# Linear attention and a mixture of experts on one core: running sums over token pairs, the low part of the second input on GpSimd, and queues in a new order

## The reference

```
x = x + layernorm(attention(layernorm(x)))          # 16 heads of 8
x = x + layernorm(experts(layernorm(x)))            # one shared expert, the best 2 of 8 others

attention:  q, k, v = x @ W_qkv + b                 # q, k through elu + 1
            for each token t of a sequence:
              kv += k_t (outer) v_t;  ks += k_t     # 8 x 8 per head
              out_t = (q_t @ kv) / (q_t . ks + 1e-6)
            return out @ W_out + b_out
experts:    shared = gelu(x @ Wfc_s + b) @ Wproj_s + b
            p = softmax(x @ Wr); top 2, gates scaled to sum to 1
            return shared + sum over the two of gate * (gelu(x @ Wfc[e] + b) @ Wproj[e] + b)
```

## Time and profile before

| | us |
|---|---|
| median of 3 runs | 409.97 |
| lowest and highest | 406.25, 412.97 |
| the profiled execution, its own time | 410.09 |
| its span, first to last instruction | 408.3 |
| busy: TensorE, VectorE, ScalarE, GpSimd | 348.2, 285.7, 264.1, 258.4 |

### The profile page before, as it was taken

How to read it: one execution, slowest core, us unless ns; L and a number is a source line. 1 busy time by engine, 2 the same in 40 slices (tenths; PEclk the granted TensorE clock), 3 DMA queues, 4 the chain that set the end, 5 groups by cost and what they waited for, 6 DMA issues and landing times.

```text
span 408.3 us, 8196 instructions
## 1 busy us (share of the span) xinstructions
PE 348.2 (85%) x2523; PEld 299.0 (73%) x2530; DVE 285.7 (70%) x685; ACT 264.1 (65%) x700; POOL 258.4 (63%) x328
## 2 busy tenths in 40 slices
PE   7888498989878999888998839499999998998884
PEld 3447257887766878766787839389989998998863
DVE  4989488998978889987944504176554538777666
ACT  4959266796976859786536733256655558678665
POOL 8786675657849587593885556466654555486650
PEclk9969979999999989999899977789999999999999
DMA  6577455574462504234067325299977869988317
GB/s 201 160 210 199 86 159 112 116 210 118 136 177 70 162 27 141 79 95 127 28 189 228 106 94 171 77 245 259 310 219 226 252 223 350 308 282 244 119 55 206
DMA packets 53521, 69.17 MB, mean 169 GB/s; under 512 B 6365, under 2 KB 37386, under 8 KB 53482
## 3 DMA queue, kind: packets, MB, share of 16 engines
q1 hardware_dynamic: 47556, 58.58, 50.0%
q0 software_dynamic: 4544, 9.35, 6.6%
q10 hardware_dynamic: 1382, 0.79, 0.7%
HBM read 40.06 MB, written 18.15 MB: 143 GB/s over the span
## 4 chain that ended last, share of the span: by engine, by line
PE 35%; ACT 17%; another core or an unknown queue 11%; DVE 10%; issue 8%; POOL 6%; POOLq 1%; DVEq 0%; ACTq 0%
PE bO L1302 6%; PE bS L1523 5%; PE bA L1274 4%; PE bO L1523 4%; ACT hs L1127 3%; ACT L1018 2%; DVE w_lo L2078 2%; ACT shared L899 2%; ACT shared L891 1%; DVE SH L2027 1%; PE bT L1352 1%; POOL KV L705 1%; POOL expert_lists L681 1%; PE bV L1496 1%
## 5 line engine op out<-in xcount | busy, mean ns | idle before, releaser
L797 POOL DMA_INDIRECT expert_results<-yb,yrow x78 | 79.6, 1020 | 62.0 <-DVE yb L2110 35.8
L681 POOL DMA_INDIRECT expert_lists<-rows,pos x64 | 63.1, 985 | 23.0 <-issue 23.0
L1673 DVE TENSOR_TENSOR_SCAN KV<-bS,KV 128x1024 f32<-128x1024 bf16 x32 | 72.9, 2282 | 4.8 <-POOL KV L705 4.5
L1302 PEld LDWEIGHTS bO<-wout_rot,Z 128*128 128x128 f32 x512 | 59.8, 192 | 10.7 <-POOL Z L762 4.6
L1302 PE MATMUL bO<-wout_rot,Z 128*128 128x128 f32 x512 | 62.8, 277 | 5.7 <-POOL Z L762 2.0
L1127 ACT ACTIVATE hs<-bV,KV 128x256 f32<-128x256 f32 x56 | 22.0, 476 | 22.4 <-remote 9.8
L2102 DVE COPY yrow<-xb 128x2 int32<-128x2 int32 x24 | 5.2, 217 | 43.2 <-PE bS L1523 15.4
L1523 PE MATMUL bO<-KV,hs 128*128 128x128 f32 x232 | 30.8, 288 | 1.7 <-ACT hs L1127 1.7
L1274 PE MATMUL bA<-w2s_sb,hs 128*128 128x128 f32 x224 | 30.7, 289 | 0.0
L1523 PEld LDWEIGHTS bO<-KV,hs 128*128 128x128 f32 x232 | 28.8, 201 | 2.6 <-ACT hs L1127 2.5
L1274 PEld LDWEIGHTS bA<-w2s_sb,hs 128*128 128x128 f32 x224 | 28.7, 204 | 0.1
(11 more groups left out here) (371 smaller groups left out, 989.2 us busy)
## 6 DMA issues: line engine op xcount, KB each, us to landing
KV<-packed_weights SPq DMA_DIRECT2D x21, 578.0 KB
Z<-packed_weights SPq DMA_DIRECT2D x18, 578.0 KB
xb<-expert_lists SPq DMA_DIRECT2D x39, 129.0 KB
vr<-vr SPq DMA_DIRECT2D x16, 224.0 KB, 2.5
shared<-expert_results SPq DMA_DIRECT2D x7, 512.0 KB, 6.1
vr<-vr SPq DMA_DIRECT2D x16, 192.0 KB
vr<-vr SPq DMA_DIRECT2D x16, 160.0 KB
vr<-vr SPq DMA_DIRECT2D x16, 128.0 KB
```

The lines of the kernel that those rows point to most:

```text
L681: g.indirect_dma_start(out=lists, out_offset=bass.IndirectOffsetOnAxis(ap=pos[:, m:m + 1], axis=0), in_=rows[:, m // TILES, m % TILES, :], ...
L797: g.indirect_dma_start(out=results, out_offset=bass.IndirectOffsetOnAxis(ap=yrow[n][:, c], axis=0), in_=yb[n][:, c, :], in_offset=None).th ...
L1302: ins = t.matmul(bO[:, j * D:(j + 1) * D], Z[:, d, j * P:(j + 1) * P], wout_rot[:, d], start=False, stop=True, skip_group_check=True)
L1673: v.tensor_tensor_scan(w, ps_keep, w, 0.0, ALU.mult, ALU.add).then_inc(s["kv_sum"], 1)
```

## The change

- **Running sums over token pairs.** A scan now runs over 128 elements: its state takes in the even token of a pair and then the odd one, and is written at the odd token. The two operands are the even and the odd products, both in SBUF. One pair of diagonals takes four scans. `SUMS` has a column of zeros ahead of each sequence, and `sums_at(d)` reads for the tokens 2m and 2m + 1 the places 2m - 1 and 2m + 1. So an even token gets the sum up to the pair before it and lacks its own term, the same for all diagonals: (q . k) of its head times v. `own_terms` multiplies q and k of the even tokens, `own_sums` on TensorE adds up the features of a head (a matmul with `same_head`, 256 columns), `own_values` multiplies by v, and `own_added` adds the result to Z0. A reduction makes `same_head` once; the constants of `ps_keep` go.
- **Z2** moves from GpSimd to VectorE, and Z products are made one diagonal at a time. `out_part` takes diagonal 1 first, then 2 and 3, 0, 4 and 5, 6, 7.
- **Low part.** GpSimd subtracts `xt2_hi` from `xt2` (`rest_of_input`). The matmul and the copy on ScalarE go, and `fc` uses the low part last.
- **Rows.** The normalized rows are written straight into one of two row sets that alternate (`rows_of_step[i % 2]`), and `rows_of` copies once instead of twice, now between the second and the third gelu.
- **Order.** GpSimd makes the last key products ahead of the scatters; its eight scatters of a step are split 2, 3 and 3. ScalarE takes `squares_of_x1` ahead of `copy_queries`. Semaphores are shared out anew.

The core of the diff:

```diff
-        KV = sb("KV", [P, E, STEP])
+        SUMS = sb("SUMS", [P, E, STEP // L, L + 1])
+        KV = SUMS[:, :, :, 1:]
+        own = sb("own", [P, STEP // L, L // 2])
...
+        def evens(w):
+
+            return w.rearrange("p s (m o) -> p s m o", o=2)[:, :, :, 0]
+
+        def sums_at(d):
+
+            part = SUMS[:, d]
+            return bass.AP(part.tensor, part.offset, [part.ap[0], part.ap[1], [2, L // 2], [2, 2]])
+
+        def by_twos(w):
+
+            return w.rearrange("p (s m o) -> p s m o", s=STEP // L, o=2)
...
+            AT_END = 5
...
+            def rest_of_input(i):
+
+                pool.wait_ge(s["xt2_high"], i)
+                g.tensor_tensor(xt2_lo[:], xt2[:], xt2_hi[:].bitcast(F32), ALU.subtract).then_inc(s["xt2_lo"], 1)
...
-                if head and routed:
-                    route_gaps(i)
-                    route_chosen(i)
-                if from_on(i, 3) and head:
-                    scatters(i - 1, before_next(i - 1), 2 * TILES)
                 if isinstance(i, int) and i == 0:
                     means_late()
                 if head and not (isinstance(i, int) and i == 1):
                     last_pairs(i)
-                if not head:
-                    scatters(i - 1, before_next(i - 1), 2 * TILES)
+                if head and routed:
+                    route_gaps(i)
+                    route_chosen(i)
+                if i >= 3:
+                    scatters(i - 1, AT_END, 2 * TILES)
...
-                    g.tensor_tensor(Z[:, 0], KV[:, 0], qn[:], ALU.mult).then_inc(s["z0_ready"], 1)
+                    g.tensor_tensor(by_twos(Z[:, 0]), sums_at(0), by_twos(qn[:]), ALU.mult).then_inc(s["z0_ready"], 1)
...
-                    g.tensor_tensor(Z[:, 1], KV[:, 1], qn[:], ALU.mult).then_inc(s["z1_ready"], 1)
+                    g.tensor_tensor(by_twos(Z[:, 1]), sums_at(1), by_twos(qn[:]), ALU.mult).then_inc(s["z1_ready"], 1)
+                if tail and head:
+                    inv_std2(i)
...
-                if head:
-                    pool.wait_ge(s["kv_sum"], 4 * i + 2)
-                    g.tensor_tensor(Z[:, 2], KV[:, 2], qn[:], ALU.mult).then_inc(s["z1_ready"], 1)
...
-                if routed:
-                    scatters(i, 0 if head else 1, before_next(i) if head else 2 * TILES)
+                if head and routed:
+                    scatters(i, 0, 2)
+                if head and tail:
+                    rest_of_input(i)
+                if head and routed:
+                    scatters(i, 2, AT_END)
+                if not head:
+                    scatters(i, 1, 2 * TILES)
...
+                rows = rows_of_step[i % 2]
+                a.activation(rows[:, 1, :, 0:D], rows[:, 0, :, 0:D], ACT.Copy)
...
-                normal(2, lambda j: xn2[:, j], lambda j: Xt(i - 1, j), "xn2_ready", i)
+                    act.wait_ge(s["t2_done"], i - 2)
+                    act.wait_ge(s["rows_ready"], i - 2)
+                set_free(act, i - 1)
+                normal(2, lambda j: rows_of_step[(i - 1) % 2][:, 0, j, 0:D], lambda j: Xt(i - 1, j), "xn2_ready", i)
...
-                    gelus(i - 2, 0, CH, pair_h)
+                    gelus(i - 2, 0, 2, pair_h)
+                    rows_of(i)
+                    gelus(i - 2, 2, CH, pair_h)
...
+                if tail:
+                    squares_of_x1(i)
                 copy_queries(i)
+                if nxt and routed:
+                    a.activation(warm[:], one8, ACT.Exp)
                 if routed:
...
-                    act.wait_ge(s["t2_done"], i)
+                    second_input(i)
                     if from_on(i, 2):
                         act.wait_ge(s["fc_done"], CH * (i - 1))
-                    a.activation(xt2_hi[:], bT[:], ACT.Copy)
-                    second_input(i)
...
-                t.matmul(bank[:], hi, xt2_lo[:], start=True, stop=False)
-                t.matmul(bank[:], hi, xt2_hi[:], start=False, stop=False)
-                t.matmul(bank[:], lo, xt2_hi[:], start=False, stop=True).then_inc(s["fc_done"], 1)
+                if c == 0:
+                    pe.wait_ge(s["xt2_high"], st + 1)
+                t.matmul(bank[:], hi, xt2_hi[:], start=True, stop=False)
+                t.matmul(bank[:], lo, xt2_hi[:], start=False, stop=False)
+                if c == 0:
+                    pe.wait_ge(s["xt2_lo"], st + 1)
+                t.matmul(bank[:], hi, xt2_lo[:], start=False, stop=True).then_inc(s["fc_done"], 1)
...
+            def own_sums(st):
+
+                pe.wait_ge(s["own_ready"], st + 1)
+                t.matmul(bS[:, 0:STEP // 2], same_head[:].rearrange("p e h -> p (e h)"),
+                         own[:].rearrange("p s m -> p (s m)"), start=True, stop=True).then_inc(s["own_summed"], 1)
+
             def out_part(st, part):
                 if part == 0:
-                    pe.wait_ge(s["z0_ready"], st + 1)
-                if part in (1, 2):
-                    pe.wait_ge(s["z1_ready"], 2 * st + part)
-                if 1 < part < 5:
-                    pe.wait_ge(s["z_ready"], 3 * st + part - 1)
-
-                for d in ((0,), (1,), (2, 3), (4, 5), (6,), (7,))[part]:
+                    pe.wait_ge(s["z1_ready"], st + 1)
+                if 0 < part < 5:
+                    pe.wait_ge(s["z_ready"], 3 * st + min(part, 3))
+                if part == 2:
+                    pe.wait_ge(s["z0_whole"], st + 1)
+
...
+                if head:
+                    own_sums(i)
                 if nxt:
                     project(i + 1)
...
-                w = KV[:, 2 * part:2 * part + 2].rearrange("p a t -> p (a t)")
-                v.tensor_tensor_scan(w, ps_keep, w, 0.0, ALU.mult, ALU.add).then_inc(s["kv_sum"], 1)
+                for d in (2 * part, 2 * part + 1):
+                    for q in range(STEP // L):
+                        two = KV[:, d, q].rearrange("p (m o) -> p o m", o=2)
+                        ins = v.tensor_tensor_scan(two[:, 1], two[:, 0], two[:, 1], 0.0, ALU.add, ALU.add)
+                ins.then_inc(s["kv_sum"], 1)
+
+            def own_terms(i):
+
+                dve.wait_ge(s["qn_copied"], i + 1)
+                v.tensor_tensor(own[:], evens(seqs(qn[:])), evens(seqs(keys)), ALU.mult).then_inc(s["own_ready"], 1)
+
+            def own_values(i):
+
+                dve.wait_ge(s["own_summed"], i + 1)
+                v.tensor_tensor(own[:], ps_own, evens(seqs(vr[:, 0])), ALU.mult).then_inc(s["own_scaled"], 1)
+
+            def own_added(i):
+
+                dve.wait_ge(s["own_scaled"], i + 1)
+                dve.wait_ge(s["z0_ready"], i + 1)
+                v.tensor_tensor(evens(seqs(Z[:, 0])), evens(seqs(Z[:, 0])), own[:], ALU.add).then_inc(s["z0_whole"], 1)
 
...
-                first = 2 * part if part > 1 else 3
-                n = 2 * part + 2 - first
-                v.tensor_tensor(Z[:, first:first + n], KV[:, first:first + n],
-                                bK[:].unsqueeze(1).broadcast_to([P, n, STEP]), ALU.mult).then_inc(s["z_ready"], 1)
+                for d in (2 * part, 2 * part + 1):
+                    ins = v.tensor_tensor(by_twos(Z[:, d]), sums_at(d), by_twos(bK[:]), ALU.mult)
+                ins.then_inc(s["z_ready"], 1)
...
                     sums(i, 2)
+                    own_terms(i)
                     if routed:
                         route_place(i)
                     if tabled:
                         table_in(0, 0, EARLY)
                     sums(i, 3)
+                    own_values(i)
+                    own_added(i)
                     zed(i, 1)
                     if again:
                         zed(i, 2)
+                    if again:
+                        zed(i, 3)
                     if routed:
                         route_pos(i)
-                    if again:
-                        zed(i, 3)
```

169 lines of the change are left out of this document (76 added, 93 removed).

## The result

| | kernel before | changed kernel |
|---|---|---|
| median, us (4 runs each) | 409.81 | 430.74 |
| lowest and highest | 406.25, 412.97 | 429.83, 431.52 |
| span of the profiled execution | 408.3 | 429.2 |

The ratio is 1.054 (95% interval 1.047 to 1.061): slower by 20.9 us. I had forecast 423, with a range up to 430. All ratios in this document leave out the executions that lie over 1.5% above the fastest of their kernel, so they can differ from the quotient of two medians.

The account below looks back on a forecast made before the run. No engine is full; each step is a ring of hand-overs between engines. Terms 6 + 4.5 + 1 + 3.2 + 0.5 - 1.5 = 13.7 on 409.97 us gave a forecast of 423 us, range 416 to 430.

Parts of the forecast that it names:

- my sum of 13.7: Whole kernel: 6 for step 0, 4.5 step 1, 1 step 2, 3.2 middle steps, 0.5 step 7, -1.5 end, in us.
- step 2: TensorE sets its 22.7 us; own_sums now stands in the queue before the projections and waits for own_terms: +1 us.
- step 7: Last step before the end: the same as in step 2, own_sums ahead in TensorE's queue, +0.5 us.
- the middle steps: Steps 3 to 6: each ends at 25.6 us against a mean of 24.8, +0.8 each, +3.2 in all.
- the port: VectorE instructions with two SBUF inputs and GpSimd instructions reading SBUF exclude each other for a whole instruction, so new scans wait.
- whole instructions taking turns: VectorE beside GpSimd: each new scan waits for the end of one running GpSimd product, then the next product waits.
- Steps 0 and 1: First steps: projections and output products wait for sums and own_terms; +6 us in step 0, +4.5 in step 1.
- The queue position: TensorE gets no projection out before own_sums; step 0's projections end at 34 us or later, not 29.
- End: Step 8 and entry to the expert blocks: low part's wait 2.0 and copy 0.6 go, subtraction 1.2 comes: -1.5 us.
- rival 2: Two stalls after step 8 (9.16, 12.14 us) shrink by more than half while rival 1 (no port wait) holds: 398 us, chance 0.10.
- Rival 3: Turns go against VectorE every time, eight us in step 0 and 26.1 in the middle steps: +20, 431 us, chance 0.08.

Follow-up runs that it names:

- the kernel with the SBUF factor: The kernel before with the scan factor of ones and zeros read from SBUF instead of PSUM; 445.12 us, ratio 1.088 to the kernel before.
- the kernel with full sums: The changed kernel with the kernel before's 1024-element scans, factor in PSUM, no own terms or own_sums; 376.91 us, ratio 1.001 to before (again: 379.34, 1.012).

## Why the prediction was right and wrong

The direction and its reason were right. The loss of 20.9 us is 7.2 above my sum of 13.7, and the time is 0.7 above the range. The step that failed is the sum: two terms for what own_sums holds up in TensorE's queue were far too small, +1 for step 2 (measured +2.8) and +0.5 for step 7 (+3.3). They make 4.6 of the 7.2 us, and moving own_sums behind the projections took 2.4 us off step 2 and 3.8 off step 7. The rest is 1.2 in the middle steps, 0.8 in the first two, with a reduction of 1.87 us that had no term, and 0.6 at the end.

- **Direction, and the port.** Right. Without own terms 128 scans take 656 ns each on average, and 401 with one operand in PSUM. The Trainium skill, SBUF — State Buffer, section "Who interferes with whom", which I had weighed against the earlier trace rows, holds for a scan too: by that rule the time was to come out slower, by its absence at 409.
- **How the turns fall.** Right in part. I had read "whole instructions taking turns" from the earlier trace rows. Steps 0 to 2 show that: one product, one instruction of VectorE. In steps 3 to 6 the last sums lose to two products in a row, and in the kernel with the SBUF factor to five instructions. For the middle steps it made little difference, since I had let the scans lose to both Z0 and Z1: I had the sums end near 17.6 and Z2 and Z3 at 19.5 after the transposes, and in step 3 they end at 17.8 and 19.7. Measured +4.4 for +3.2. Letting Z0 wait for the last sums is worth 10.3 us, of which only about 2.5 lie in these steps.
- **Steps 0 and 1.** +11.3 for +10.5. Forecast: projections end at 34 or later; they end at 36.4. The queue position is as said (8.21 us of wait). The reduction for same_head (1.87 us) has no term. It is named in my part on the change, but not priced: I took it for set-up, and did not ask whether VectorE has idle time there. In the kernel with full sums the first two steps end 2.0 us sooner without it.
- **Step 2.** A size: +2.8 for +1. own_sums waits 2.00 us, and the two projections behind it take 1.91 and 1.71 us, not 1.02, the granted clock of the step being 0.93. Moving own_sums takes 2.4 us off. I had priced the wait and not the slower matmuls behind it.
- **Step 7.** The worst term: +3.3 for +0.5. "The same" was no argument. Only this step has table operations with two SBUF inputs beside the key products (0.19 to 2.25 us), and table transposes in the queue behind own_sums (VectorE waits 2.06). I had read own_sums' queue for the projections alone. With own_sums moved step 7 is 3.8 us shorter; the table operation takes 0.19 again there, since it no longer meets the key products.
- **End.** -0.9 for -1.5. The two stalls after step 8 are 8.36 and 11.97 us (9.16 and 12.14 in the earlier trace rows), so nothing of rival 2.
- **Rivals.** Rival 3, turns against VectorE each time, gave 431 and had 0.08. The measured 430.74 is its size, but not its case: the reduction, step 2 and step 7 make up the difference, and the middle steps took 25.9 on average, between the forecast's 25.6 and its 26.1. That it fits so well is chance. The earlier trace rows hold both outcomes (1.78 us for VectorE's operation, up to 1.72 for GpSimd's products).
- **The range.** My own ends (first steps 9.9 to 13.6, middle steps 1.6 to 5.2) add up to 421.5 to 428.8, so 416 and 430 were not worked out from them; rival 3 is 428.8 by the same ends, and 13.7 on 409.97 is 423.7. Terms that I left out or rounded down could only add, so the upper end was too near.

## What to carry to other kernels

Before a VectorE instruction is given its second SBUF input, look at what GpSimd does beside it, and count at least one of its instructions, at worst the whole run without a pause (five here); one operand in PSUM took the clash away, and a wait that lets the short one go first may pay. For every instruction that is put into a queue, list all that stands behind it in every step, the odd ones too (here the table's transposes), and price TensorE's work behind a wait at the lower clock too (1.91 us instead of 1.02 for a projection here). Ask of an added set-up instruction whether its engine has idle time just there.

## What the hardware showed that I had not expected

- GpSimd's indirect transfers are held up by a VectorE scan with two SBUF inputs: in the two kernels with the factor in SBUF 0.96 us becomes 2.1 to 2.9.
- A VectorE operation of 40 elements on two SBUF inputs took 2.25 us beside one GpSimd product of 2.34; a GpSimd operation of 0.2 us took 2.17 beside a scan.
- One program takes 374 to 377 us on some chips and 409 to 413 on others. Of these 39 us 8 lie in steps 0 to 7 (204.7 and 212.5 to the last transposes) and 31 in the expert blocks, which take 166 us or 197. Busy times of the kernel before in the same stretch, first where it is slow, then where it is fast:

```profile
240.00:270.00 30.00, 17.39 (x114) 15.54 (x115) 11.51 (x53) 9.68 (x20) 17.15 (x18) 0.70 0.45 128
```
```profile
240.00:270.00 30.00, 27.93 (x241) 27.16 (x240) 17.69 (x56) 16.63 (x40) 22.99 (x24) 1.00 1.00 276
```

On the one the transfers move 128 GB/s and all engines idle, in the stalls of the earlier trace rows; on the other they move 276, and from there on VectorE has no stall above 3 us. What holds the transfers up stays open. Ratios held across the chips to about 2%, differences in us less well.
